# One block for load, first norm, router and first feed-forward, with the gate weights turned as bf16 parts

## The chip, the cores and the metric

The kernel runs on one core of a Trainium2 chip. The metric is the device time of one execution in microseconds (us); lower is better. The kernel before takes 1775.18 us in the median of three runs (1761.94, 1775.18 and 1776.92). One execution was taken with the hardware profiler; its own time is 1773.67 us.

## What is computed

Two transformer-like layers on x of 16 x 256 x 128 floats, 4096 rows (tokens) of 128. Only the first lines of it are touched here:

```python
xn = layernorm(x)
x = x + attn0(xn) + ffn0(xn)          # layer 0
...
# ffn0: 8 experts, hidden size 64 each (512 together), the two best experts per row
logits = xn @ router_w + router_b
w, idx = top_k(softmax(logits), 2); w = w / sum(w)
mask[row, idx] = w                                # 8 gate weights per row, six of them 0
h1 = gelu(einsum('btd,nde->btne', xn, W1) + b1)
out = sum over n of (einsum('btne,nef->btnf', h1, W2) + b2) * mask
```

`attn0` is a third-order linear attention with 16 heads of 64; layer 1 (norm, attention with relative positions, a capacity-limited expert layer) follows. Nothing of these is changed.

## The kernel before

The program is written engine by engine; each engine runs its list in order and waits on semaphores. A `Block` ends with a barrier of all five engines, so no instruction of a stage starts before the stage ahead has ended. Order is set by hand alone; there is no scheduler. The 4096 rows are 32 tiles of 128 (`NT`), taken in 8 groups of 4 tiles (`NG`, `TPG`, `GT` = 512 rows). `xnT_all` holds the normed rows turned, 128 features on the partitions.

Four stages touch the change, in this order:

1. `constants` (from line 76). POOL makes identity, masks and index rows; SP issues three loads (line 86): all of x as one transfer of 2 MB, and two router matrices.
2. `norm_stage` (from 114). DVE waits for all three loads, then takes the statistics of 32 tiles (line 151) in a loop, 9 small steps on 128x32 values, with a square root by ACT (186) between. Then a loop over pairs of groups: DVE norms 8 tiles (172), PE turns them (206), ACT copies the turned group out of PSUM (192), PE multiplies it with the router (212), POOL copies it to `xnT_all` (228), and DVE copies the logits (178). DVE norms the next pair only after it has copied this pair's logits.
3. `ffn0_stage` (from 282). After the barrier SP loads the feed-forward's weights (313 to 318); DVE, ACT and PE wait for all five. PE computes the first group's hidden values (379, one product of 512 columns for each of 4 chunks of 128 hidden units). DVE finds the two best experts of all rows (`top2_steps`, 249 to 274, and 332 to 341) in one chain on 128x256 values, each step waited for. Then 8 groups: ACT writes every gate weight 64 times beside each other (`wx`, 363), PE turns it once for the bias product (385) and 16 times for the four chunks (392), so that the PSUM tile `ps_w` holds each hidden unit's gate weight; ACT applies Gelu (369), DVE multiplies (347), PE computes the next group's hidden values (379) and then the outputs: for each tile 4 products with W2 (401) and one with b2 (403). DVE adds them to x (350).
4. `attn0_stage`: its first product is line 586.

A product with float32 operands is issued as two passes, so 4 products of line 379 are 8 rows in the trace; a transpose (206, 385, 392) is one.

## Time and profile before

| what | value |
|---|---|
| median of three runs | 1775.18 us |
| profiled execution, its own time | 1773.67 us |
| its span, first to last instruction | 1772.1 us |
| PE busy | 1612.4 us, 91% |
| granted TensorE clock, mean | 0.974 |
| start of the first product of `attn0_stage` | 181.59 us |

The profile page gives busy time by engine (PE is TensorE's matmuls, PEld its weight loads, DVE VectorE, ACT ScalarE, POOL GpSimd, SP the queue that issues the transfers), the span in 40 slices of 44.3 us, and groups of instructions. The timeline lists instructions in order of time, neighbours of one line merged. The windows view gives busy time and granted clock of chosen stretches. A duration is of one execution.

### The profile page before, as it was taken

To read this page: it belongs to the slowest core of one execution; us is meant where nothing else is said; L and a number is where in the kernel's file an instruction comes from. 1 tells how busy PE (TensorE), PEld (TensorE's weight loads), DVE (VectorE), ACT (ScalarE), POOL (GpSimd) and SP (SyncE) were. 2 spreads that over 40 slices of the span, in tenths; PEclk is the share of its full clock that TensorE was granted. 3 is DMA by queue.
4 is the path that set the end of the run, shared out by engine and by line. 5 is a ranking of instruction groups with operands and counts; after the bars stand their busy time and mean duration, and the time that the engine had idled before them with its cause. 6 is when DMAs were issued, how large, how long until landed. Compare 5 with 4: busy or idle time off the path is not lost. (4 is left out here: it accounts for less than half of the span.)

```text
span 1772.1 us, 39751 instructions
## 1 busy us (share of the span) xinstructions
PE 1612.4 (91%) x14552; PEld 1267.3 (72%) x14552; DVE 917.8 (52%) x3198; ACT 752.9 (42%) x2111; POOL 297.4 (17%) x377
## 2 busy tenths in 40 slices
PE   3599999999999999999959999977999999999995
PEld 3366788888888888888835656645777777777774
DVE  3322554545454545454532222225777777777774
ACT  1232122222222222222222222228887888887873
POOL 1000220010111111110052000001232233233222
PEclk9999899999999999999979999998999999999998
DMA  1200750000000000000024233218888888888886
GB/s 48 63 0 0 73 102 19 4 10 6 7 4 7 6 5 6 5 6 7 7 89 132 73 106 107 77 62 237 254 229 244 247 232 251 247 238 224 242 239 178
DMA packets 230781, 181.43 MB, mean 102 GB/s; under 512 B 82591, under 2 KB 219641, under 8 KB 230640
## 3 DMA queue, kind: packets, MB, share of 16 engines
q1 hardware_dynamic: 225266, 167.14, 35.0%
q0 software_dynamic: 5376, 12.44, 2.4%
q8 instruction: 87, 1.43, 0.3%
q14 instruction: 52, 0.43, 0.1%
HBM read 103.60 MB, written 75.78 MB: 101 GB/s over the span
## 5 line engine op out<-in xcount | busy, mean ns | idle before, releaser
L769 DVE TENSOR_TENSOR a0MT<-a0ps_M,mask 128x384 f32<-128x384 f32 x256 | 142.5, 557 | 223.2 <-PE a0ps_M L614 223.2
L1542 ACT ACTIVATE a1Pm<-a1Pm,a1nmx 128x256 f32<-128x256 f32 x512 | 255.7, 505 | 0.8 <-DVE a1nmx L1604 0.8
L1604 DVE CUSTOM_DVE_ANT_0 a1Pm<-a1ps_S,a1Sb 128x256 f32<-128x256 f32 x512 | 196.2, 420 | 88.6 <-issue 84.8
L722 ACT ACTIVATE a0oT<-a0ps_o 128x256 f32<-128x256 f32 x128 | 49.1, 383 | 441.3 <-PE a0ps_o L626 326.1
L1537 ACT ACTIVATE a1Rt<-a1ps_R 128x384 f32<-128x384 f32 x264 | 128.7, 487 | 113.1 <-PE a1ps_R L1402 93.5
L1421 PE MATMUL a1ps_T<-ident,a1Pm 128*128 128x128 f32 x1024 | 156.6, 275 | 0.0
L1157 DVE TENSOR_TENSOR f1hid<-f1ge,f1ps_b 128x512 f32<-128x512 f32 x80 | 54.9, 687 | 193.7 <-PE f1ps_b L1090 186.2
L612 PE MATMUL a0ps_M<-a0AT 128*128 128x256 f32 x512 | 153.7, 382 | 1.2 <-DVE a0AT L764 1.2
L764 DVE TENSOR_TENSOR a0AT<-a0ps_A,mask 128x384 f32<-128x384 f32 x256 | 130.8, 552 | 39.4 <-PE a0ps_A L595 39.4
L586 PE MATMUL a0ps_qk<-xnT_all,a0w_in 128*128 (+1 forms) x512 | 146.6, 409 | 1.4 <-PEq L310 1.4
L1402 PE MATMUL a1ps_R<-rel_st,a1stk 72*128 72x192 bf16 x528 | 90.0, 253 | 45.2 <-ACT a1Rt L1537 24.1
L712 ACT ACTIVATE a0qk<-a0ps_qk 128x512 f32<-128x512 f32 x128 | 76.3, 596 | 96.6 <-PE a0ps_qk L586 96.6
L1421 PEld LDWEIGHTS a1ps_T<-ident,a1Pm 128*128 128x128 f32 x1024 | 115.5, 142 | 0.4 <-issue 0.2
L586 PEld LDWEIGHTS a0ps_qk<-xnT_all,a0w_in 128*128 128x128 f32 x512 | 87.7, 191 | 30.3 <-issue 23.3
L613 PEld LDWEIGHTS a0ps_M<-a0AT 128*128 128x128 f32 x512 | 97.6, 191 | 13.3
L1100 PE MATMUL f1ps_o<-f1wo,f1hid 128*128 128x128 f32 x768 | 91.5, 280 | 15.4 <-DVE f1hid L1157 15.4
L1100 PEld LDWEIGHTS f1ps_o<-f1wo,f1hid 128*128 128x128 f32 x768 | 88.6, 195 | 19.5 <-DVE f1hid L1157 11.9
L1411 PE MATMUL a1ps_S<-a1stk 72*128 72x256 bf16 x512 | 101.3, 280 | 0.0
L1088 PE MATMUL f1ps_a<-f1xT,f1w 128*128 128x512 f32 x192 | 99.3, 599 | 0.7 <-ACT f1xT L1120 0.7
L1542 ACT ACTIVATION_READ_ACCUMULATOR a1Pm<-a1Pm,a1nmx 128x1 f32 x512 | 99.9, 195 | 0.0
L614 PE MATMUL a0ps_M<-a0AT 128*128 128x128 f32 x512 | 99.2, 276 | 0.0
L613 PE MATMUL a0ps_M<-a0AT 128*128 128x128 f32 x512 | 98.6, 274 | 0.0
(242 smaller groups left out, 3009.1 us busy)
## 6 DMA issues: line engine op xcount, KB each, us to landing
skew<-a1Rt SPq DMA_DIRECT2D x132, 384.0 KB, 5.3
a1Sb<-skew SPq DMA_DIRECT2D x131, 384.0 KB, 5.4
a1stk<-parts SPq DMA_DIRECT2D x153, 64.0 KB
a1stk<-parts SPq DMA_DIRECT2D x51, 192.0 KB
parts<-a1prt SPq DMA_DIRECT2D x18, 384.0 KB, 5.6
f1w<-in_L_ffn_w_kernel SPq DMA_DIRECT2D x16, 344.0 KB, 3.0
f1w<-in_L_ffn_w_kernel SPq DMA_DIRECT2D x16, 320.0 KB, 3.3
f1wo<-in_L_ffn_wo_kernel SPq DMA_DIRECT2D x16, 320.0 KB, 4.4
```

Source lines behind the costliest of these rows:

```text
L586: ins = nc.tensor.matmul(ps_qk[:, i, :], w_in[:, i, p * P:(p + 1) * P], xnT_all[:, bass.ds(b * T, T)], start=True, stop=True)
L612: nc.tensor.matmul(ps_M[h][:, 0:T], AT[h][:, 0:P], AT[h][:, 0:T], start=True, stop=True)
L613: nc.tensor.matmul(ps_M[h][:, T:HB], AT[h][:, P:T], AT[h][:, P:T], start=True, stop=False)
L764: nc.vector.tensor_tensor(AT[h][:, :], ps_A[h][:, 0:HB], mask[:, :], ALU.mult).then_inc(A_ready, 1)
L769: nc.vector.tensor_tensor(MT[i][h][:, :], ps_M[h][:, 0:HB], mask[:, :], ALU.mult).then_inc(M_ready, 1)
L1088: nc.tensor.matmul(ps_a[u % 2][:, :], w[i][:, u * P:(u + 1) * P], xT[i][:, :], start=True, stop=True).then_inc(a_done, 1)
L1100: ins = nc.tensor.matmul(ps_o[i][:, s, :], hid[:, c, s * P:(s + 1) * P], wo[i][:, c, :], start=(c == 0), stop=(c == HC - 1))
L1411: ins = nc.tensor.matmul(ps_S[hp % 2][:, n, :], stk[par][:, 0, h, it * P:(it + 1) * P], stk[par][:, 1, h, :], start=True, stop=True)
L1421: ins = nc.tensor.transpose(ps_T[k % 2][:, n, jt, :], Pm[:, place(2 * k + n), jt * P:(jt + 1) * P], ident[:, :])
L1537: nc.scalar.activation(Rt[:, hp, :, :], ps_R[:, :, :].rearrange("p n c -> p c n"), ACT.Copy).then_inc(sm["R_ready"], 1)
L1542: nc.scalar.activation(Pm[:, place(h), :], Pm[:, place(h), :], ACT.Exp, bias=nmx[it][:, h:h + 1], scale=-1.0, accum_out=den[it][:, h:h + 1 ...
L1604: nc.vector.tensor_tensor_reduce(out=Pm[:, place(h), :], in0=ps_S[hp % 2][:, n, :], in1=bias_of(it, hp, n), scale=-1.0, scalar=3.0e38, op0 ...
```

## The change

Four functions are replaced by one, `front_stage`, in one `Block`:

- x is loaded in four transfers of 8 tiles; the statistics of a quarter wait for that quarter alone. Routers, gate bias, b1, W1, W2 and b2 are issued right behind x by SP. b2 is loaded nine times into a cleared tile (three copies of 8 rows in each of three blocks of 32 partitions).
- All loops are written out. In the norm, the order on PE is: turn group g, then the router products of group g-1; ACT copies the turned group straight to `xnT_all`; the router's results of all 32 tiles stay in one PSUM tile. POOL has no part in it.
- Of the softmax only the difference of the two largest logits goes through exp; the two weights are 1/(1+e) and e/(1+e).
- DVE splits the gate weights into three bf16 parts (`pw`, 128 columns a tile), and b2 likewise (`b2s`). PE turns `pw` by a bf16 product with a bf16 identity (357), ACT copies the result as bf16 (`wT`, 318), and PE repeats each weight over its expert's hidden rows by one bf16 product of 512 columns per chunk with a 0/1 matrix `esel` (364). The bias product (375) is bf16 with all 128 rows.
- In a group PE does two repeats, two hidden products of the next group, two repeats, two hidden products, the turning of the next group's weights, and the outputs.

The float32 products with W1 and W2, Gelu, the multiplication by DVE and the addition to x stay.

```diff
-def constants(nc, ident, mask, iota_e, ltri, ones_bf, group_base, one, load, loaded):
...
-def norm_stage(nc, x_all, xn_all, xnT_all, ident, router, logits, tag, loaded=None, loads=0):
...
-def top2_steps(nc, v, done, soft, iota_e, m, tag, exp_start, exp_done):
...
-def ffn0_stage(nc, x_all, xnT_all, logits, router_b, W1, b1, W2, b2, ident, iota_e, attn_load, attn_loaded, load_tables):
...
+KPARTS = 3
...
+def front_stage(nc, a, x_all, xnT_all, ident, mask, iota_e, ltri, ones_bf, group_base, one, router, attn_load, attn_loaded, load_tables):
+    XL = 4
+    TPL = NT // XL
+    SMALL = 4 + KPARTS * KPARTS
...
+        pw = m.sb("f0pw", [P, NT, 4, P // 4], BF16)
+        wT = [m.sb(f"f0wT{i}", [P, GT], BF16) for i in range(2)]
...
+        ps_l = ps_y[:, :, :].rearrange("p j d -> p (j d)")[:, 0:NT * E].rearrange("p (t e) -> p t e", e=E)
+            @block.sync
+            def _(sp):
+                x_dram = a["L0_attn_x"].rearrange("b (t p) d -> p (b t) d", p=P)
+                for q in range(XL):
+                    sp.dma_start(x_all[:, q * TPL:(q + 1) * TPL, :], x_dram[:, q * TPL:(q + 1) * TPL, :]).then_inc(x_in[q], 16)
+                sp.dma_start(router[:, 0, :], a["L0_ffn_router_w"]).then_inc(small, 16)
+                sp.dma_start(router[:, 1, :], a["L1_ffn_router_w"]).then_inc(small, 16)
+                sp.dma_start(rb[:, :], a["L0_ffn_router_b"].partition_broadcast(P)).then_inc(small, 16)
+                sp.dma_start(b1c[:, :], a["L0_ffn_b1"].rearrange("(c e) f -> (e f) c", e=EPC), allow_slow_non_contiguous=True).then_inc(small, 16)
+                sp.dma_start(w1[:, :, :].rearrange("p c (e f) -> p (c e) f", e=EPC),
+                             a["L0_ffn_W1"].rearrange("e d f -> d e f")).then_inc(weights, 16)
+                sp.dma_start(w2[:, :, :], a["L0_ffn_W2"].rearrange("e f d -> (e f) d").rearrange("(c p) d -> p c d", p=P)).then_inc(weights, 16)
+                sp.wait_ge(b2_clear, 1)
+                for j in range(KPARTS):
+                    for k in range(KPARTS):
+                        sp.dma_start(b2f[j * 32 + k * E:j * 32 + (k + 1) * E, :], a["L0_ffn_b2"]).then_inc(small, 16)
+                for dst, src in attn_load:
+                    sp.dma_start(dst, src).then_inc(attn_loaded, 16)
+                load_tables(sp)
...
+                for k in range(KPARTS):
+                    pool.wait_ge(cs, 5 + k)
+                    nc.gpsimd.affine_select(out=esel[:, :, :, :], in_=esel[:, :, :, :], compare_op=ALU.not_equal, fill=1.0,
+                                            base=-E * k, pattern=[[-EPC, FC0], [-1, EPC], [0, FF0 // E]], channel_multiplier=1).then_inc(cs, 1)
+                nc.gpsimd.tensor_copy(ident_bf[:, :], ident[:, :]).then_inc(cs, 1)
...
+            @block.vector
+            def _(v):
+                def nstep(n, ins):
+                    ins.then_inc(norm_step, 1)
+                    v.wait_ge(norm_step, NT + n)
+                for q in range(XL):
+                    v.wait_ge(x_in[q], 16)
+                    for t in range(q * TPL, (q + 1) * TPL):
+                        nc.vector.bn_stats(stats[:, t:t + 1, :], x_all[:, t:t + 1, :]).then_inc(norm_step, 1)
+                v.wait_ge(norm_step, NT)
...
+                for g in range(NG):
+                    if g > 1:
+                        v.wait_ge(xT_done, g - 1)
+                    for j in range(TPG):
+                        t = g * TPG + j
+                        ins = nc.vector.tensor_scalar(xn[g % 2][:, j, :], x_all[:, t, :], mean[:, t:t + 1], rstd[:, t:t + 1],
+                                                      ALU.subtract, ALU.mult)
+                    ins.then_inc(xn_ready, 1)
+                v.wait_ge(small, 16 * SMALL)
+                nc.vector.tensor_copy(b2p[:, :], b2f[:, :]).then_inc(b2_step, 1)
+                v.wait_ge(b2_step, 1)
...
+                v.wait_ge(lg_done, NG)
+                v.wait_ge(cs, 4)
+                gstep(1, nc.vector.tensor_tensor(wt[:, :, :], ps_l, bc(rb[:, :], 1, NT), ALU.add))
+                src = wt
...
+                v.wait_ge(pw_clear, 1)
+                src = wt
+                for k in range(KPARTS):
+                    ins = nc.vector.tensor_copy(pw[:, :, 0:KPARTS, k * E:(k + 1) * E], bc(src[:, :, :], 2, KPARTS))
+                    if k < KPARTS - 1:
+                        gstep(19 + 2 * k, ins)
+                        gstep(20 + 2 * k, nc.vector.tensor_tensor(rest[:, :, :], src[:, :, :], pw[:, :, 0, k * E:(k + 1) * E], ALU.subtract))
+                        src = rest
+                    else:
+                        ins.then_inc(pw_ready, 1)
...
+                act.wait_ge(small, 16 * SMALL)
+                def keep_h(g, c):
+                    act.wait_ge(h_done, g * FC0 + c + 1)
+                    if g > 0:
+                        act.wait_ge(hw_ready, (g - 1) * FC0 + c + 1)
+                    nc.scalar.activation(h[:, c, :], ps_h[c][:, :], ACT.Gelu, bias=b1c[:, c:c + 1]).then_inc(h_ready, 1)
+                def keep_wT(g):
+                    act.wait_ge(wT_done, g + 1)
+                    if g > 1:
+                        act.wait_ge(y_done, g - 1)
+                    nc.scalar.activation(wT[g % 2][:, :], ps_g[:, :], ACT.Copy).then_inc(wT_kept, 1)
+                for c in range(FC0):
+                    keep_h(0, c)
+                keep_wT(0)
+                for g in range(NG):
+                    if g < NG - 1:
+                        for c in range(FC0):
+                            keep_h(g + 1, c)
+                        keep_wT(g + 1)
+            @block.tensor
+            def _(pe):
+                def turn_x(g):
+                    pe.wait_ge(xn_ready, g + 1)
+                    if g > 1:
+                        pe.wait_ge(xT_ready, g - 1)
+                    for j in range(TPG):
+                        ins = nc.tensor.transpose(ps_w[g % 2][:, j * P:(j + 1) * P], xn[g % 2][:, j, :], ident[:, :])
+                    ins.then_inc(xT_done, 1)
+                def route(g):
+                    pe.wait_ge(xT_ready, g + 1)
+                    for j in range(TPG):
+                        t = g * TPG + j
+                        ins = nc.tensor.matmul(ps_l[:, t, :], xnT_all[:, t * P:(t + 1) * P], router[:, 0, :], start=True, stop=True)
+                    ins.then_inc(lg_done, 1)
+                def hidden(g, cs):
+                    for c in cs:
+                        if g > 0:
+                            pe.wait_ge(h_ready, (g - 1) * FC0 + c + 1)
+                        nc.tensor.matmul(ps_h[c][:, :], w1[:, c, :], xnT_all[:, g * GT:(g + 1) * GT], start=True, stop=True).then_inc(h_done, 1)
+                def turn_weights(g):
+                    if g > 0:
+                        pe.wait_ge(wT_kept, g)
+                    for j in range(TPG):
+                        parts = pw[:, g * TPG + j, :, :].rearrange("p j c -> p (j c)")
+                        ins = nc.tensor.matmul(ps_g[:, j * P:(j + 1) * P], parts, ident_bf[:, :], start=True, stop=True)
+                    ins.then_inc(wT_done, 1)
+                def repeat_weights(g, cs):
+                    for c in cs:
+                        if c >= 2 or g > 0:
+                            pe.wait_ge(hw_ready, g * FC0 + c - 1)
+                        nc.tensor.matmul(ps_w[c % 2][:, :], esel[:, c, :, :].rearrange("p e f -> p (e f)"), wT[g % 2][:, :],
+                                         start=True, stop=True).then_inc(w_done, 1)
+                def outputs(g):
+                    pe.wait_ge(hw_ready, (g + 1) * FC0)
+                    if g > 0:
+                        pe.wait_ge(y_added, g)
+                    for j in range(TPG):
+                        rows = slice(j * P, (j + 1) * P)
+                        for c in range(FC0):
+                            nc.tensor.matmul(ps_y[:, j, :], hw[:, c, rows], w2[:, c, :], start=(c == 0), stop=False)
+                        ins = nc.tensor.matmul(ps_y[:, j, :], wT[g % 2][:, rows], b2s[:, :], start=False, stop=True)
+                    ins.then_inc(y_done, 1)
+                pe.wait_ge(cs, 3)
+                for g in range(NG):
+                    turn_x(g)
+                    if g == 1:
+                        pe.wait_ge(small, 16 * SMALL)
+                    if g > 0:
+                        route(g - 1)
+                route(NG - 1)
+                pe.wait_ge(weights, 16 * 2)
+                hidden(0, range(FC0))
+                pe.wait_ge(cs, 9)
+                pe.wait_ge(pw_ready, 1)
+                turn_weights(0)
+                pe.wait_ge(b2_step, 2 * KPARTS)
+                for g in range(NG):
+                    pe.wait_ge(wT_kept, g + 1)
+                    repeat_weights(g, (0, 1))
+                    if g < NG - 1:
+                        hidden(g + 1, (0, 1))
+                    repeat_weights(g, (2, 3))
+                    if g < NG - 1:
+                        hidden(g + 1, (2, 3))
+                        turn_weights(g + 1)
+                    outputs(g)
```

The order on PE in the norm. Before (names ending in 0 and 1 are the two buffers), the loop's body, run three times after a first copy of it:

```order
L206 MATMUL n0ps_t0<-ident,n0xn0 128x128 x4
L204 REGISTER_ALU
L206 MATMUL n0ps_t1<-ident,n0xn1 128x128 x4
L212 MATMUL n0ps_l0<-router,n0xT0 128x8 x4
L212 MATMUL n0ps_l1<-router,n0xT1 128x8 x4
L72 REGISTER_ALU
L72 COMPARE_AND_BRANCH
```

After, the start of the list:

```order
L336 MATMUL f0ps_w0<-ident,n0xn0 128x128 x4
L336 MATMUL f0ps_w1<-ident,n0xn1 128x128 x4
L343 MATMUL f0ps_y<-router,xnT_all 128x8 x4
L336 MATMUL f0ps_w0<-ident,n0xn0 128x128 x4
L343 MATMUL f0ps_y<-router,xnT_all 128x8 x4
L336 MATMUL f0ps_w1<-ident,n0xn1 128x128 x4
```

Between the turning of a group and its router products now stands the turning of the next.

One group of the feed-forward on PE. Before, the loop's body:

```order
L385 MATMUL f0ps_t<-ident,f0wx 8x128 x4
L392 MATMUL f0ps_w<-ident,f0wx 128x128 x8
L389 ISA
L392 MATMUL f0ps_w<-ident,f0wx 128x128 x4
L389 REGISTER_ALU
L392 MATMUL f0ps_w<-ident,f0wx 128x128 x4
L378 REGISTER_ALU
L379 ISA
L379 MATMUL f0ps_h<-xnT_all,f0w 128x512 x4
L401 MATMUL f0ps_y<-f0w,f0hw 128x128 x4
L403 MATMUL f0ps_y<-f0b,f0wT 128x128
```

After:

```order
L364 MATMUL f0ps_w<-f0wT,f0esel 128x512 x2
L350 MATMUL f0ps_h<-xnT_all,f0w 128x512 x2
L364 MATMUL f0ps_w<-f0wT,f0esel 128x512 x2
L350 MATMUL f0ps_h<-xnT_all,f0w 128x512 x2
L357 MATMUL f0ps_g<-f0ident_bf,f0pw 128x128 x4
L374 MATMUL f0ps_y<-f0w,f0hw 128x128 x4
L375 MATMUL f0ps_y<-f0b2s,f0wT 128x128
```

Four products of 512 columns stand in the place of 20 transposes, and the hidden products stand between them. The last two rows come four times in both.

## Rows read from the trace of the kernel before

**Rows 1.** Page: busy time of each engine and its share of the span.
```profile
PE 1612.4 (91%) x14552; PEld 1267.3 (72%) x14552; DVE 917.8 (52%) x3198; ACT 752.9 (42%) x2111; POOL 297.4 (17%) x377
```
**Rows 2.** Windows, stretch by stretch: length, busy us (instructions) by engine, clock, DMA.
```profile
0.00:22.21 22.21, 0.00 (x0) 0.00 (x0) 9.51 (x42) 1.51 (x2) 2.82 (x17) 1.00 0.35 95
22.21:51.62 29.41, 21.50 (x96) 19.68 (x96) 10.37 (x40) 4.78 (x8) 4.87 (x8) 1.00 0.00 0
51.62:57.48 5.86, 0.00 (x0) 0.00 (x0) 0.01 (x1) 1.28 (x1) 0.00 (x0) 1.00 0.63 157
57.48:69.66 12.18, 5.41 (x8) 2.08 (x8) 10.69 (x29) 0.42 (x1) 0.00 (x0) 0.92 0.52 150
69.66:86.50 16.84, 13.19 (x69) 9.49 (x70) 2.57 (x4) 8.11 (x8) 0.00 (x0) 0.85 0.01 4
86.50:164.99 78.49, 71.92 (x410) 51.44 (x409) 19.55 (x30) 28.63 (x36) 0.00 (x0) 1.00 0.00 0
164.99:181.59 16.60, 13.25 (x62) 10.73 (x61) 3.95 (x6) 2.86 (x5) 0.03 (x1) 0.66 0.00 0
280.00:880.00 600.00, 600.00 (x4548) 511.15 (x4548) 308.56 (x911) 147.32 (x369) 56.87 (x76) 1.00 0.02 6
```
**Rows 3.** Timeline of a pair of groups in the norm: start, us, engine, line.
```profile
37.13 2.24 DVE L172 TENSOR_SCALAR n0xn<-x_all,n0mean,n0rstd 128x128 f32 x8 [0.59 <-issue]
38.39 2.15 PE L206 MATMUL n0ps_t<-ident,n0xn 128*128 128x128 f32 x8 [2.19 <-DVE n0xn L172]
40.19 3.48 PEld L212 LDWEIGHTS n0ps_l<-router,n0xT 128*128 128x128 f32 x16
```
**Rows 4.** Timeline: the last load of the feed-forward and the wait for it.
```profile
54.14 0.63 SPq L318 DMA_DIRECT2D f0b<-in_L_ffn_b  x1
57.48 0.42 DVE L332 TENSOR_TENSOR f0wt<-logits,f0rb 128x256 f32<-128x256 f32 x1 [5.86 <-DMA f0b<-in_L_ffn_b]
57.94 0.42 DVE L249 TENSOR_REDUCE f0mx<-f0wt 128x32 f32<-128x256 f32 x1
```
**Rows 5.** Timeline: eight of the first group's transposes.
```profile
72.23 1.72 PEld L392 LDWEIGHTS f0ps_w<-ident,f0wx 128*128 128x128 f32 x8
```
**Rows 6.** Windows by clock level, columns as in rows 2.
```profile
57.50:60.90 3.40, 3.40 (x4) 1.51 (x5) 2.75 (x7) 0.42 (x1) 0.00 (x0) 1.00 1.02 381
67.80:74.60 6.80, 2.73 (x12) 2.09 (x12) 1.64 (x5) 3.79 (x4) 0.00 (x0) 0.50 0.11 20
74.70:170.20 95.50, 85.60 (x488) 61.38 (x489) 25.38 (x39) 35.71 (x46) 0.00 (x0) 1.00 0.00 0
```
**Rows 7.** Timeline of a group in the steady part, and of the last.
```profile
155.57 3.68 PE L379 MATMUL f0ps_h<-xnT_all,f0w 128*128 x8
160.48 1.16 PE L401 MATMUL f0ps_y<-f0w,f0hw 128*128 128x128 f32 x8
161.57 0.48 PE L403 MATMUL f0ps_y<-f0b,f0wT 8*128 8x128 f32 x2
174.71 2.08 PE L401 MATMUL f0ps_y<-f0w,f0hw 128*128 128x128 f32 x8
176.71 0.79 PE L403 MATMUL f0ps_y<-f0b,f0wT 8*128 8x128 f32 x2
```
**Rows 8.** Timeline of the start.
```profile
1.95 5.89 SPq L86 DMA_DIRECT2D router<-in_L_ffn_router_w  x2
11.70 1.96 DVE L151 BATCH_NORM_STATS2 n0stats<-x_all  x8 [11.70 <-DMA router<-in_L_ffn_router_w]
20.10 0.21 DVE L154 TENSOR_TENSOR n0mean<-n0stats 128x32 f32<-128x32 f32 x1
```
**Rows 9.** Groups by line: a cast from float32 to bf16 on DVE.
```profile
L884 DVE CAST t1parts<-t1rpad 8x384 bf16<-8x384 f32 x1 | 0.3, 348 | 0.0
```
**Rows 10.** Timeline: bf16 products of the later attention, 256 columns each.
```profile
1501.43 0.39 PE L1411 MATMUL a1ps_S<-a1stk 72*128 72x256 bf16 x2
1501.66 0.33 PE L1402 MATMUL a1ps_R<-rel_st,a1stk 72*128 72x192 bf16 x2
```

More of the change, by code:

```diff
@@ L1837, in program @@
                 mask = g.sb("mask", [P, T + P])
-                logits = g.sb("logits0", [P, NT, E])
-                x_dram = a["L0_attn_x"].rearrange("b (t p) d -> p (b t) d", p=P)
-                load = [(x_all[:, :, :], x_dram), (router[:, 0, :], a["L0_ffn_router_w"]), (router[:, 1, :], a["L1_ffn_router_w"])]
-                x_loaded = g.sem("x_loaded")
                 w_in0 = g.sb("a0w_in", [P, 3, H0 * DK])
@@ L1844, in program @@
                 w_loaded = g.sem("a0loaded")
-                constants(nc, ident, mask, iota_e, ltri, ones_bf, group_base, one, load, x_loaded)
-                norm_stage(nc, x_all, None, xnT_all, ident, router[:, 0, :], logits, "n0", x_loaded, len(load))
                 attn_load = [(w_in0[:, i, :], a["L0_attn_W_" + n]) for i, n in enumerate("qkv")]
                 attn_load.append((w_out0[:, :, :], a["L0_attn_W_o"].rearrange("(c p) d -> p c d", p=P)))
-                ffn0_stage(nc, x_all, xnT_all, logits, a["L0_ffn_router_b"], a["L0_ffn_W1"], a["L0_ffn_b1"], a["L0_ffn_W2"],
-                           a["L0_ffn_b2"], ident, iota_e,
-                           attn_load, w_loaded, load_tables)
+                front_stage(nc, a, x_all, xnT_all, ident, mask, iota_e, ltri, ones_bf, group_base, one, router, attn_load, w_loaded,
+                            load_tables)
                 attn0_stage(nc, a, x_all, xnT_all, xn_all, w_in0, w_out0, w_loaded, mask, one, zeros, ident, router[:, 1, :], iota_e, ltri,
```

414 lines of the change are left out of this document (132 added, 282 removed).

## The prediction

> **What bounds the kernel now.** The page comes first: PE is busy for 91% of the span [rows 1], but this share is a mean over stages, so the second view is the table of stretches [rows 2]. In it a reader is to see two different kernels. From 280 to 880 us, in the first attention, PE is busy for all of 600 us: what starts this stage earlier ends it earlier. The stretch ahead of it, up to 181.59 us, is the one that the change rewrites, and there PE is busy for about 125 us (the sum of its column). So the change is priced by the time at which line 586 starts, and nothing behind that line is expected to move by itself.
>
> The stretches also say what waits. For 22.21 us PE does nothing: a load, statistics, small steps. In 22.21 to 51.62 the norm holds every engine below 75%: the four pairs of groups take 7.35 us each [rows 2], made of 1.26 us of DVE alone (37.13 to 38.39), 2.15 us of transposes and 3.48 us of router products, and the next pair starts only behind them [rows 3]. Then 5.86 us of waiting for the feed-forward's loads [rows 4], 12.18 us of gating on DVE, 16.84 us for the first group, 78.49 us for six groups (13.08 each) with PE busy for 92%, and 16.60 us for the last group and the barrier [rows 2].
>
> **The clock on the way.** The clock column reads 1.00 in the norm, but the durations don't: 16 router passes take 3.48 us, 0.218 each [rows 3], as the transposes do at 72.23, 8 in 1.72 us or 0.215 each, in a stretch granted 0.50 [rows 5, 6]. In the stretch at 1.00 an output pass takes 0.136 (8 from 160.48 to 161.57) [rows 6, 7]. I read the norm as run at the lower level (1.2 GHz), and take the column there as not recorded (it reads 1.00 from 57.50 to 60.90 too, with passes of 0.85 us [rows 6]).
>
> **Start to first normed tile: 22.21 us before, 15.8 after.** The statistics waited for all of x and two routers until 11.70; the last began 0.5 us before the steps at 20.10, so 32 took 8.4 us [rows 8]. In quarters, three quarters of them hide under the transfer. The last quarter lands at 11.7 at the latest, and its 8 take 1.96 us. The small steps, 20.10 to 22.21, stay 2.1 us: fewer waits, same chain through ACT. Sum 15.8.
>
> **Norm and router, up to the gating's first step: 57.48 before, 39.0 after.** PE starts 1.26 us behind DVE as before. A group costs it 4 transposes at 0.215 and 8 router passes at 0.218, 2.6 us; DVE needs 1.1 us for a group (half of 2.24), ACT 0.6 (4.78 us for 8) [rows 2, 3], and both now work under PE, since the turning of the next group stands between. Eight groups: 20.8 us. POOL's copies and DVE's logits copies go; none of them was late, so they count as nothing.
> PE's first router product now waits for all 13 small loads. Before, SP's two router transfers, issued behind x, occupied it until 7.84 [rows 8]. Behind them stand four others of 0.33 to 0.57 us and nine of b2; one of b2 took 0.63 [rows 4], so nine take 6.1 us at that price and the last is issued at 15.8. Before, the last load landed 2.7 us behind its issue (54.77 to 57.48) [rows 4]: 18.5. PE asks for it at 15.8 + 1.26 + 1.7 = 18.8. I charge 1 us of waiting; zero is the lower end, and the upper end is the second rival. The load wait of 5.86 us is gone, and b2's splitting (9 DVE steps near 0.2 us) lies under the last two groups of PE. Sum 15.8 + 1.26 + 20.8 + 1.0 + 0.1 = 39.0; gain 18.5.
>
> **Gating: 12.18 before, 10.5 after.** Steps of 128x256 follow each other in 0.46 us (57.48, 57.94) [rows 4]. The new chain has 17 of them, about 1.0 us of 128x32 steps, and three casts of 768 elements. A cast of 384 took 0.348 [rows 9] and a step of 256 0.42; a cast of 768 lies between 0.5 (by the cast's slope) and 0.95 (by twice a step of 384 without its start-up). I take 0.55, the cast being the nearest row. 7.8 + 1.0 + 1.65 = 10.5, gain 1.7; with the upper end 0.5. ACT's exp lies under four DVE steps. The first hidden products lie under the gating, as before.
>
> **First group: 16.84 before, 12.9 after.** Turning and copying the weights: about 0.5 for four bf16 products, 0.6 for the copy (ACT's 128x512 copies in the norm) [rows 2], hops 0.3: 1.4 in place of 1.9 us for `wx` and what follows it. PE has then been idle and starts at the lower level: two repeats near 0.43 each, four hidden passes at 0.85 (4 in 3.40 us from 57.50 on) [rows 6]: 4.3. The clock then rose both times after about 3 us of unbroken work, 57.50 to 60.9 and 71.6 to 74.6 [rows 6]. The rest at the upper level, 7.2 (next part). Gain 3.9.
>
> **Six groups: 78.5 before, 56.5 after.** At the upper level eight hidden passes take 3.68 us with the tail of the last, 0.43 each or 3.44 [rows 7]. The outputs cost 1.09 us for 8 passes of line 401 (160.48 to 161.57) and about 0.41 for the two of line 403 (0.48 with the tail), 1.5 a tile, 6.0 a group. The bf16 bias product is one pass. Two bf16 products of 256 columns begin and give way in 0.23 us [rows 10], so 512 columns cost 0.23, with 0.86 (two float32 passes) as the upper end; the bias product of 128 columns I put at 0.1, between 0.06 and 0.41 likewise. So: repeats 0.92, hidden 3.44, turning 0.3, outputs 4 x 1.19 = 4.76; 9.4 a group. The 20 transposes and PE's waits for DVE go; the window of six groups holds 6.6 us of idle PE, 1.1 a group [rows 2]. Nothing takes their place: DVE needs 3.3 us a group (19.55 us in six) [rows 2] and ACT 3.0 (five steps of 0.6), and the hidden products stand where PE waited. Their cover is wide: DVE's four multiplications (0.65 each in the same window) end about 0.4 us ahead of the outputs. Gain 22.0.
>
> **Last group and barrier: 16.60 before, 13.4 after.** No hidden products to hide DVE: its addition and four multiplications, 3.7 us. Before, the clock fell in this group, and a tile of outputs took 2.0 us for eight passes (174.71 to 176.71) and 0.7 for two [rows 7]. I expect that again: 2.0 + 0.15 for a tile, 8.3 in all (the first tile partly at the upper level), and the same 1.4 us to line 586. Gain 3.2.
>
> **Sum.** 18.5 + 1.7 + 3.9 + 22.0 + 3.2 = 49.3 us. Line 586 moves from 181.6 to 132.3. Against the profiled execution's own 1773.7: **1724 us**. That execution is 1.5 us below the median of the three runs, which differ by 15 us among themselves.
>
> **Rivals.**
> *The clock rises in the norm.* Its PE list is now unbroken. Against: in each pair before, 5.6 us without a gap (2.15 of transposes, then 3.48 of router passes of 8 columns) didn't raise it [rows 3], whereas 2.8 us of mostly transposes at 71.6 did [rows 6]; so router passes seem to count for little, and they are two thirds of the new list. For: the pairs had a gap of 2 us, the new list has none. It would save half of what is left after some 4 us, 8.4 us, but DVE's 1.1 us a group then sets the pace: gain 57, 1717 us.
> The Trainium skill ("TensorE: Matmul & The Clock Gate", section "What's actually happening") says that the clock follows how busy PE has recently been and does not count instructions. By that rule this rival is the forecast, at 1717; the pairs of the norm speak against it as far as they go.
>
> *The nine loads of b2 hold SP.* The two router transfers took 2.9 us each on SP with x in flight [rows 8]. At that price nine take 26.5 us, 20 more than charged, and all of it falls on PE, which has only two groups to turn before it waits: gain 29, 1745 us. Against: x has landed at 11.7, and the queue should be free after that; so at worst a part.
>
> *The clock stays low through the feed-forward.* This ends above the time before. At the lower level a group costs 4 x 0.43 + 8 x 0.85 + 0.45 + 4 x 2.15 = 17.6 us in place of 9.4: six groups lose 49, the first group's second half 7; gain 49 - 56, 1781 us. It decides from about six groups at that level. It would need PE to look less busy with single-pass products of 0/1 weights than with transposes. Against: with gaps of over 1 us a group it was granted 1.00 for 95.5 us without a break [rows 6], and the new list has fewer.
>
> *Written-out code is read late*, or the longer chains meet a wait not seen here: no row shows a stall of this kind; it belongs to the small remainder.
>
> **Chances.** Forecast 0.62, clock in the norm 0.19, loads 0.13, low clock 0.04, unnamed 0.02. The range reaches from the first rival, less some spread of runs, to most of the second: **1709 to 1740 us**. A measurement of this kernel can tell about 1% (18 us). Faster by more: 0.62 + 0.19 + 0.13 = 0.94. The low clock ends half within 1% and half above, with half of the unnamed each: 0.03 and 0.03.
>
> **What would show it.** The first product of the attention near 132 us. Normed tiles from 15.8 us; one group of the norm every 2.6 us on PE (1.1 to 1.3 if the clock rises). No wait of PE for a load over 1 to 2 us. From the last router product to the turning of weights 10.5 us. Groups every 9.4 us without a wait of PE; one of 17 would be the low clock. From line 586 on, the same 1590.5 us as before (1772.1 - 181.6). I am wrong if groups take over 11 us at full clock, since then the bf16 products cost what float32 ones do, or if the rest of the span gives back part of the gain.

## The result, and the profile after

The changed kernel takes 1711.03 us in the median of four runs (1698.71 to 1715.68); the kernel before 1773.51 (four runs). The ratio is 0.9647, with a 95% interval of 0.9587 to 0.9706: 3.5% faster. The profiled execution took 1715.68 us, its span is 1714.1, 58.0 us less than before. The forecast was 1724 (1709 to 1740).

The page's busy row, to be read against [rows 1]: TensorE's work fell by 28 us, the span by 58, so half of the gain is idle time.

```profile
span 1714.1 us, 39121 instructions
PE 1584.3 (92%) x14424; PEld 1247.7 (73%) x14424; DVE 920.5 (54%) x3193; ACT 741.9 (43%) x2103; POOL 299.4 (17%) x376
```

The windows of the changed kernel, cut where its stages change: start; norm and router; gating; first group; six groups; last group and barrier. Columns as in [rows 2], whose stretches they answer to.

```profile
0.00:14.40 14.40, 0.00 (x0) 0.00 (x0) 7.96 (x41) 1.51 (x2) 9.19 (x24) 1.00 0.78 186
14.40:35.83 21.43, 20.17 (x97) 19.77 (x98) 10.48 (x41) 6.06 (x9) 0.00 (x0) 1.00 0.37 107
35.83:46.29 10.46, 5.13 (x8) 1.88 (x8) 9.62 (x24) 3.94 (x6) 0.00 (x0) 0.98 0.00 0
46.29:58.58 12.29, 11.48 (x55) 7.27 (x56) 2.57 (x4) 3.83 (x6) 0.00 (x0) 0.74 0.00 0
58.58:109.76 51.18, 51.18 (x314) 36.60 (x312) 19.01 (x30) 19.42 (x30) 0.00 (x0) 1.00 0.00 1
109.76:120.32 10.56, 7.28 (x43) 5.86 (x41) 3.81 (x6) 0.00 (x0) 0.01 (x1) 0.84 0.00 0
```

The last window ends at 120.32, where attention's first product starts (line 568 now). The reader is to see that TensorE is busy without a gap for the six groups (51.18 of 51.18 us, before 71.92 of 78.49). It is idle where VectorE's chain stands alone (the start, 5.4 us of the gating, 2.0 us of the last group), for 0.8 us behind ScalarE's first copy of the weights, and for 1.3 us at the barrier. The timeline of TensorE shows one group of the norm, and most of a steady group (start, us, line):

```profile
19.22 1.09 PE L336 MATMUL f0ps_w<-ident,n0xn 128*128 128x128 f32 x4
20.11 1.71 PE L343 MATMUL f0ps_y<-router,xnT_all 128*128 128x8 f32 x8
...
58.64 0.59 PE L364 MATMUL f0ps_w<-f0wT,f0esel 128*128 128x512 bf16 x2
59.07 1.88 PE L350 MATMUL f0ps_h<-xnT_all,f0w 128*128 128x512 f32 x4
60.79 0.59 PE L364 MATMUL f0ps_w<-f0wT,f0esel 128*128 128x512 bf16 x2
61.22 1.88 PE L350 MATMUL f0ps_h<-xnT_all,f0w 128*128 128x512 f32 x4
62.94 0.39 PE L357 MATMUL f0ps_g<-f0ident_bf,f0pw 128*128 128x128 bf16 x4
63.16 1.11 PE L374 MATMUL f0ps_y<-f0w,f0hw 128*128 128x128 f32 x8
64.11 0.22 PE L375 MATMUL f0ps_y<-f0b2s,f0wT 128*128 128x128 bf16 x1
64.16 1.11 PE L374 MATMUL f0ps_y<-f0w,f0hw 128*128 128x128 f32 x8
```

Start to start, a group of the norm is 2.45 us (19.22 to 21.67); an output tile is 1.00 us (63.16 to 64.16), of which 0.95 are the eight float32 passes and 0.05 the bf16 bias product. In the kernel before the same tile took 1.50 [rows 7].

Behind 120.32 not all is as it was. From attention's first product to the end the changed kernel takes 1593.8 us (1714.1 - 120.32), the one before 1590.5. By stage, before and after: first attention 730.4 and 739.0, second feed-forward 277.7 and 275.1, second attention 582.5 and 579.7. (A stage is counted from its first product to that of the next; the second feed-forward's is the transpose that waits for its gathered rows, the second attention's the first that reads `a1stk`.) So 61.3 us were won ahead of the attention and 3.3 given back. The experiments take up both.

### The profile page after: what moved, and what is told of

Same layout as the page of the kernel before. It is cut to its first block and busy times, and to the rows that moved or that the text cites. A ratio compares the mean times of both kernels' runs of the same rounds, so it can differ in the third digit from the quotient of the medians.

```text
span 1714.1 us, 39121 instructions
## 1 busy us (share of the span) xinstructions
PE 1584.3 (92%) x14424; PEld 1247.7 (73%) x14424; DVE 920.5 (54%) x3193; ACT 741.9 (43%) x2103; POOL 299.4 (17%) x376
```

## The experiments

Each is one profiled execution, unless a number of runs is named. Since whole spans scatter, verdicts rest on when attention starts and on stage lengths. The first four cut the change into parts. In a diff, `...` stands for lines left out.

**The kernel before with its bias product over 128 rows.**

```diff
-        b2s = m.sb("f0b2", [E, D])
+        b2s = m.sb("f0b2", [P, D])
-        wT = m.sb("f0wT", [E, GT])
+        wT = m.sb("f0wT", [P, GT])
...
+                nc.gpsimd.memset(b2s[:, :], 0.0).then_inc(padded, 1)
+                nc.gpsimd.memset(wT[:, :], 0.0).then_inc(padded, 1)
...
```

> The kernel before, with one edit: wT and b2s have 128 rows instead of 8, cleared once, so that the bias product contracts over 128 partitions, still in float32; the result is the same. Theory A (the number of rows): a float32 product over 8 rows keeps the weight loads of its neighbours from running under it, and that is what made a tile of outputs cost 1.50 us against the 1.00 after the change. Then a tile costs about 1.07 us (ten passes at 0.107), a steady group 13.08 - 1.7 = 11.4 us, and the attention starts near 167 instead of 181.6. Theory B (the type): float32 passes next to each other cost 0.136 and a bf16 product between them is what made the others cheap. Then a tile stays at 1.5 us and the attention starts at 181.6.

Measured: attention starts at 167.33 us, where theory A had it, 14.3 earlier than in the kernel before; 1752.81 us. Its timeline, an output tile:

```profile
103.90 1.05 PE L409 MATMUL f0ps_y<-f0w,f0hw 128*128 128x128 f32 x8
104.79 0.39 PE L411 MATMUL f0ps_y<-f0b,f0wT 128*128 128x128 f32 x2
105.01 1.06 PE L409 MATMUL f0ps_y<-f0w,f0hw 128*128 128x128 f32 x8
```

A tile falls from 1.50 to 1.11 us with the same number of passes and more data: the bias product takes 0.22 in place of 0.41 (start to start), and the eight passes behind it 0.89 in place of 1.09. The 8-row product cost twice, once itself and once in its neighbours. This is what the forecast of the output tiles lacked. A steady group takes 11.64 us (92.26 to 103.90) in place of 13.08, so eight groups account for 11.5 of the 14.3 us. In the last group the clock fell later (1.00 up to 160 us, 0.77 from there to 167.3; before, 0.50 to 0.52 from 170 us to attention's start); what this part is worth was not separated.

**The changed kernel with float32 transposes and an 8-row float32 bias product, as before, in place of the bf16 parts.**

```diff
-                        ins = nc.tensor.matmul(ps_g[:, j * P:(j + 1) * P], parts, ident_bf[:, :], start=True, stop=True)
+                        ins = nc.tensor.transpose(ps_g[0:E, j * P:(j + 1) * P], wx[:, j, :, 0], ident[:, :])
...
-                        nc.tensor.matmul(ps_w[c % 2][:, :], esel[:, c, :, :].rearrange("p e f -> p (e f)"), wT[g % 2][:, :],
-                                         start=True, stop=True).then_inc(w_done, 1)
+                        for j in range(TPG):
+                            wide = wx[:, j, c * EPC:(c + 1) * EPC, :].rearrange("p e f -> p (e f)")
+                            ins = nc.tensor.transpose(ps_w[c % 2][:, j * P:(j + 1) * P], wide, ident[:, :])
+                        ins.then_inc(w_done, 1)
```

> The changed kernel with the bf16 parts undone: ACT widens the gate weights, PE turns them by 4 + 16 float32 transposes a group, and the bias product is float32 over 8 rows; block, loads, order and written-out loops stay. Theory A (the gain of a group is the sum of its parts): transposes 2.1 us, hidden products 3.44, outputs 6.0: 11.6 us a steady group; the gating is 2.7 us shorter without the casts; the attention starts near 143. Theory B (ACT's widening of 1.9 us comes onto the path): 12.5 to 13 us a group, near 151.

Measured: attention at 138.88 us, 1724.88 us. That is earlier than either theory gave, though the group is theory A's (11.6 us). The timeline of a group:

```profile
65.36 1.16 PE L375 MATMUL f0ps_y<-f0w,f0hw 128*128 128x128 f32 x8
66.45 0.48 PE L376 MATMUL f0ps_y<-f0b2e,f0wT 8*128 8x128 f32 x2
...
69.87 0.61 PE L356 MATMUL f0ps_g<-ident,f0wx 128*8 128x128 f32 x4
70.31 1.04 PE L365 MATMUL f0ps_w<-ident,f0wx 128*128 128x128 f32 x8
```

A group is 11.53 us against 8.53, and TensorE has no gap in it either. Of the 3.0 us, 1.9 are the four output tiles (5.90 for 4.01), and 1.1 the 20 transposes (0.44 and twice 0.88) in place of 1.08 us of bf16 products. So the bf16 parts are worth 18.6 us (138.88 - 120.32) at this place. Two thirds of a group's share come from the new bias product: by the run before, about 1.6 us from its 128 rows in place of 8 (0.39 a tile), the rest from one bf16 pass in place of two float32 ones. One third comes from fewer passes for turning and repeating.

**The changed kernel with each group's hidden products behind all four repeats, not between them.**

```diff
-                    repeat_weights(g, (0, 1))
+                    repeat_weights(g, (0, 1, 2, 3))
                     if g < NG - 1:
-                        hidden(g + 1, (0, 1))
-                    repeat_weights(g, (2, 3))
-                    if g < NG - 1:
-                        hidden(g + 1, (2, 3))
+                        hidden(g + 1, (0, 1, 2, 3))
```

> The changed kernel with one part undone: all four repeats first, then all four hidden products of the next group, as before the change. Theory A (the order is worth PE's waits): PE waits for DVE between the repeats again, 1.1 to 1.3 us a group; a steady group takes 8.53 + 1.2 = 9.7 us and the attention starts near 129 instead of 120.3. Theory B (the waits were hidden by something else): 8.5 us a group, 120 to 121.

Measured: attention at 128.22 us, 7.9 later, as theory A said; 1713.67 us. TensorE waits twice in a group, for the two PSUM tiles that VectorE still reads, and a group is 10.0 us (69.40 to 79.44). The order between the repeats is worth about 8 us.

```profile
69.40 0.38 PE L364 MATMUL f0ps_w<-f0wT,f0esel 128*128 128x512 bf16 x1
70.73 0.39 PE L364 MATMUL f0ps_w<-f0wT,f0esel 128*128 128x512 bf16 x1 [0.95 <-DVE f0hw L291]
71.33 0.39 PE L364 MATMUL f0ps_w<-f0wT,f0esel 128*128 128x512 bf16 x1 [0.21 <-DVE f0hw L291]
```

**The changed kernel with x in one transfer.**

```diff
-                for q in range(XL):
-                    sp.dma_start(x_all[:, q * TPL:(q + 1) * TPL, :], x_dram[:, q * TPL:(q + 1) * TPL, :]).then_inc(x_in[q], 16)
+                sp.dma_start(x_all[:, :, :], x_dram[:, :, :]).then_inc(x_in[0], 16)
...
```

> The changed kernel with x loaded by one transfer again; the statistics wait for all of it. Theory A (the quarters hide three quarters of the statistics): these start near 11 us instead of 5.35; 24 of them at 0.206 us, 4.9 us, come onto the path; the first tile is normed near 19.5 instead of 14.4 and the attention starts near 125.5. Theory B (the small transfers or the routers set the start): 14.4 to 15.5 and 120.3 to 121.5.

Measured: attention at 125.43 us, 5.1 later, as theory A said; 1720.44 us. The statistics (VectorE's timeline) start when all of x is there; in the changed kernel half of them are done by 8.8 us:

```profile
11.49 6.28 DVE L216 BATCH_NORM_STATS2 n0stats<-x_all 128x6 f32<-128x128 f32 x32 [11.49 <-DMA x_all<-in_L_attn_x]
```

```profile
5.35 3.43 DVE L217 BATCH_NORM_STATS2 n0stats<-x_all 128x6 f32<-128x128 f32 x16 [5.35 <-DMA x_all<-in_L_attn_x]
8.96 1.64 DVE L217 BATCH_NORM_STATS2 n0stats<-x_all 128x6 f32<-128x128 f32 x8 [0.18 <-DMA x_all<-in_L_attn_x]
10.94 1.65 DVE L217 BATCH_NORM_STATS2 n0stats<-x_all 128x6 f32<-128x128 f32 x8 [0.34 <-DMA x_all<-in_L_attn_x]
```

**The clock in the norm: 24 products that nobody reads, ahead of it.**

```diff
+                def filler(n, bank):
+                    for _ in range(n):
+                        nc.tensor.matmul(bank[:, :], fill[:, 0:P], fill[:, :], start=True, stop=True)
...
+                pe.wait_ge(x_in[2], 16)
+                filler(24, ps_h[0])
```

> The changed kernel with 24 bf16 products of 512 columns on TensorE, read by nobody, between the landing of the third quarter of x (about 9 us) and the first transpose of the norm (15.7 us). They should raise the clock before the norm begins. Theory A, that the clock follows how busy TensorE's rows are and falls again because a group's 32 router passes write 8 columns each: the first one to three groups of the norm take about 1.5 us, the rest 2.45 us as before, attention begins at 116 to 121 us (120.3 without the change). Theory B, that it stays where it is as long as TensorE has no gap: all eight groups run at VectorE's 1.3 us each (10.48 us busy over 8), the norm ends 9 us earlier, attention begins near 111 us.

Measured: attention at 111.35 us, 9.0 earlier, where theory B had it, but not quite for its reason; 1701.54 us. TensorE's timeline:

```profile
19.33 0.64 PE L339 MATMUL f0ps_w<-ident,n0xn 128*128 128x128 f32 x4
19.80 0.96 PE L346 MATMUL f0ps_y<-router,xnT_all 128*128 128x8 f32 x8
...
24.93 2.72 PE L346 MATMUL f0ps_y<-router,xnT_all 128*128 128x8 f32 x16
27.51 6.18 PE L353 MATMUL f0ps_h<-xnT_all,f0w 128*128 128x512 f32 x8
```

A group takes 1.28 us, TensorE's own work at 2.4 GHz, in place of 2.45. At 25 us the granted clock falls (1.00 from 20 to 25 us, 0.65 from 25.0 to 27.5), and TensorE's last gap, of 0.20 us, lies 8 us back. So the norm of the changed kernel did run at 1.2 GHz, as its durations said and the clock column (1.00) did not. And the fall within unbroken work speaks against theory B, by which the clock stays as long as TensorE has no gap, as six groups at the higher clock speak against theory A's one to three. A later run, of the two edits further down with 24 such products of 480 columns, lost it at 23.2 us (windows):

```profile
15.82:23.20 7.38, 7.14 (x65) 6.81 (x64) 6.78 (x27) 3.59 (x6) 0.00 (x0) 1.00 0.78 240
23.20:29.79 6.59, 6.59 (x34) 6.59 (x34) 2.27 (x12) 2.48 (x4) 0.00 (x0) 0.51 0.15 26
```

Both stretches have TensorE busy to over 96% with transposes and router passes, one at 1.00, the next at 0.51. What sets the moment of the fall is open.

**The same, and two more such products after each group of the norm.**

```diff
+                    filler(2, ps_h[1])
```

> As the run with 24 products ahead of the norm, and two more such products after each group of the norm. If columns streamed per group are what holds the clock (theory A), two products (0.43 us of 1.8 at the higher clock) may hold it up: 8 groups at 1.3 to 1.8 us, the norm and router some 14 us long in place of 21.4, attention near 113 us. If they are too few, each costs 0.43 us at the lower clock: the norm gets 7 us longer, attention begins near 127 us. Theory B of the run before: same as that run, plus 3.5 us, near 114.5 us.

Measured: the clock stays at 1.00 through the norm and the eight hidden passes behind it (3.68 us in place of 6.18); a group takes 1.68 us; attention at 113.77, where theory A had it; 1706.92 us. TensorE's timeline, the last full group and the hidden passes:

```profile
25.05 0.60 PE L339 MATMUL f0ps_w<-ident,n0xn 128*128 128x128 f32 x4
...
26.72 0.60 PE L339 MATMUL f0ps_w<-ident,n0xn 128*128 128x128 f32 x4
...
29.21 3.68 PE L353 MATMUL f0ps_h<-xnT_all,f0w 128*128 128x512 f32 x8
```

With two products of 512 columns a group, the clock stayed in this one run; with 8-column passes and transposes alone it fell in all three. The products cost 0.4 us a group, and the run before had lost the clock only near the norm's end. So its router products end 1.7 us sooner (its hidden passes start at 27.51, these at 29.21), and so does attention start sooner there.

**What was given back: GpSimd's two table subtractions, moved out of the attention.** In the changed kernel's timeline, GpSimd and VectorE at the start of attention:

```profile
121.03 8.82 POOL L542 TENSOR_TENSOR t1rvd<-t1rv 1x4088 f32<-1x4088 f32 x1
185.82 8.82 POOL L542 TENSOR_TENSOR t1rvd<-t1rv 1x4088 f32<-1x4088 f32 x1 [55.98 <-DMA rv_table<-t1rvd]
```

```profile
124.12 5.80 DVE L861 TENSOR_SCALAR t1rpad<-t1rk 8x129 f32<-8x129 f32 x1
129.96 0.28 DVE L862 TENSOR_SCALAR t1rpad<-t1rk 8x129 f32<-8x129 f32 x1
...
186.94 7.74 DVE L765 TENSOR_TENSOR n1dif<-n1stats 128x2 f32<-128x2 f32 x1
194.59 0.15 DVE L766 TENSOR_TENSOR n1m<-n1stats 128x2 f32<-128x2 f32 x1
```

Both long VectorE instructions end when GpSimd's do (129.9 and 194.6), and their twins right behind take 0.28 and 0.15 us. The view of waits from 120 to 240 us (total, times, longest) shows what it costs TensorE, which needs VectorE's masks; and the windows, that the clock is low behind each wait:

```profile
PE a0ps_M L594 <- DVE a0AT L746: 7.3, 2, 4.1
```

```profile
131.00:138.00 7.00, 6.19 (x26) 4.88 (x28) 3.75 (x10) 0.00 (x0) 0.00 (x0) 0.51 0.80 87
196.00:203.00 7.00, 6.20 (x26) 4.95 (x28) 4.32 (x12) 0.63 (x2) 0.02 (x1) 0.51 0.45 112
```

```diff
+                nc.gpsimd.tensor_tensor(tin.rvd[:, :, :], tin.rv[:, :, :], tin.rv[:, TAB - 1:TAB, :].to_broadcast([1, TAB, HD]),
+                                        ALU.subtract).then_inc(rvd_made, 1)
+                pool.wait_ge(rvd_out, 16)
+                nc.gpsimd.tensor_tensor(tin.rvd[:, :, :], tin.rv[:, :, :], tin.rv[:, 0:1, :].to_broadcast([1, TAB, HD]),
+                                        ALU.subtract).then_inc(rvd_made, 1)
```

(in `front_stage`, behind gating, with SP's two transfers of the table; both are gone from `attn0_stage`)

> The changed kernel with GpSimd's two one-partition subtractions of the value tables (8.8 us each, at 121 and 185.8 us, both inside attention) moved into the feed-forward's block, behind gating. Theory A, that such an operation holds VectorE's scalar and small-tensor instructions until it ends: VectorE's rpad step takes 0.3 us in place of 5.8 and n1dif 0.15 in place of 7.7, TensorE's waits of 3.1 and 4.1 us for them go, with the stretches at the lower clock behind them; attention from its first product to the second feed-forward takes 727 to 731 us in place of 739, and the kernel ends near 1706 us. In the feed-forward the same operation may lengthen VectorE's instructions in its place, but those that read PSUM with large tiles should hold nothing up for over 1 us in sum. Theory B, that VectorE was late for its own work and only ended at the same time by chance: attention takes 739 us as before and the time stays at 1714 to 1716 us.

Measured: the first attention takes 724.4 us in place of 739.0, both of TensorE's waits and both falls of the clock are gone; 1701.6 us. The first held instruction is back at its own time (VectorE's timeline):

```profile
124.03 0.27 DVE L867 TENSOR_SCALAR t1rpad<-t1rk 8x129 f32<-8x129 f32 x1
```

Theory A, and by more than it said. In their new place (46.30 and 56.87, 8.8 us each) they hold nothing up: VectorE's multiplications there, which read PSUM, keep 0.64 us each.

The 14.6 us are two things, and other profiles tell them apart. Three of the runs above left the subtractions in the attention and reached it at full clock: the padded bias product, the hidden products behind the repeats, and the 24 products ahead of the norm. Their VectorE was held in the same way, and TensorE waited the same 3.14 us, but there the clock did not fall behind the wait. TensorE's timeline, first in the changed kernel, then in the run with 24 products:

```profile
131.81 1.22 PE L594 MATMUL a0ps_M<-a0AT 128*128 128x256 f32 x2 [3.14 <-DVE a0AT L746]
```

```profile
122.83 0.70 PE L604 MATMUL a0ps_M<-a0AT 128*128 128x256 f32 x2 [3.14 <-DVE a0AT L756]
```

| profiles | TensorE's waits for held masks, us | granted clock behind them | first attention, us |
|---|---|---|---|
| changed kernel (two profiles, the second further down), x in one transfer, two more products a group | 6.8 to 7.5 | falls, twice | 736.5 to 739.8 |
| padded bias product, hidden products behind, 24 products ahead of the norm | 4.7 to 4.9 | 1.00 | 729.4 to 730.4 |
| tables moved (four profiles, with those further down) | none | 1.00 where they were | 724.4 to 725.9 |

The run with float32 transposes fits the middle row: its clock was partly low at attention's start (0.80 and 0.77 in the first 8 us), it waited 3.3 us for the masks and took 730.3. So the hold alone costs some 5 us, and the falls of the clock behind it some 8 more, where they come. They came in four of the seven profiles of the first two rows, with the same list of attention's instructions; why in these is open.

In the kernel before the first subtraction stood at 182.27 and held VectorE for 4.10 us, but its attention took only 730.4 us. Its last group had left TensorE at 1.2 GHz, so it reached the held mask later and didn't wait for it; at the second subtraction it waited 1.2 us. VectorE's timeline and the windows:

```profile
187.06 4.10 DVE L879 TENSOR_SCALAR t1rpad<-t1rk 8x129 f32<-8x129 f32 x1
```

```profile
181.60:188.00 6.40, 5.71 (x18) 4.07 (x19) 2.92 (x6) 0.60 (x1) 6.40 (x3) 0.50 0.49 54
```

Against 724.4, the kernel before lost 6.0 us here, to the low clock up to 190 us and to that wait, and the changed kernel 14.6, to the hold and to the clock behind it. The difference, 8.6, is the length that attention gained; the two later stages were 5.4 us shorter, which leaves the 3.3 given back.

**The changed kernel, and the one with the tables moved, five runs each.**

> The changed kernel once more, unedited, for the scatter of its time: its four executions so far gave 1698.71 to 1715.68 us. If the hold of VectorE by GpSimd sometimes ends with TensorE's clock falling behind it and sometimes not, the executions fall into two heaps, near 1700 and near 1714 us; the median between 1707 and 1714. Its profiled attention takes 726 to 731 us where the clock stays up at 131 and 196 us, and 736 to 739 where it falls.

> The changed kernel with GpSimd's two table subtractions moved into the feed-forward's block, timed five times beside the unedited one. Theory A (the hold costs TensorE 3.1 and 4.1 us of waiting, and sometimes the clock behind it): all executions near 1701 us, median 5 to 11 us below the unedited kernel's, with less scatter. Theory B (its one run was a lucky one): scatter and median as the unedited kernel's, within 2 us.

Measured: unedited, a median of 1711.41 us (1708.28 to 1714.69), ratio to before 0.9654, interval 0.9629 to 0.9679; its five times form no two heaps. Tables moved, 1701.56 (1696.72 to 1708.87), ratio 0.9611, interval 0.9584 to 0.9638. The first attention takes 739.8 us in the one profile and 725.6 in the other. The stage gain of 14 us came back; of it 10 us show in the median. Some of the unedited kernel's executions may have kept the clock up behind the waits, as three profiles above did; no run shows it, since stages are known for the profiled execution alone. The scatter did not shrink (12.2 us from lowest to highest, against 6.4), so theory A was wrong there.

**All together, to look for the fastest.** Tables moved, 24 products of 480 columns ahead of the norm, 12 in the wait for gating, 4 and 4 in the last group's waits; and a second kernel with the first two of these edits alone:

```diff
+                filler(24, ps_h[0])
...
                 hidden(0, range(FC0))
+                filler(12, ps_w[0])
...
+                    if g == NG - 1:
+                        filler(4, ps_h[0])
                     repeat_weights(g, (2, 3))
+                    if g == NG - 1:
+                        filler(4, ps_h[0])
```

> The changed kernel with both edits that worked apart, and two more: 24 products ahead of the norm; GpSimd's two table subtractions in the feed-forward's block; 12 bf16 products of 480 columns in TensorE's wait for gating (4.5 us), and 4 in each of the two waits for VectorE in the last group (0.95 and 0.85 us). Theory A, that the two gains stand at different places and add up: attention at 111.4 us by the first edit, its length 724 to 728 us by the second, and the rest 855 us: span near 1691 us. The products in gating keep the clock up into the first group (11.5 us there, 8.5 in a steady group: up to 2.5 us less), those in the last group spare its stretch at the lower clock (up to 1.7 us): attention near 108 us, the kernel at 1687 to 1690 us. Theory B, that the clock falls somewhere later all the same and takes back what was won: 1696 to 1702 us, no better than either edit alone.

> The run before without the 12 and the 4 and 4 products: only the 24 products ahead of the norm and the two table subtractions moved. Theory A: attention at 111.4 us and a span of 1690 to 1694 us; the difference to the run before, 2 to 4 us at attention's start, is what the clock costs in the first and the last group. Theory B: attention at 111.4 us, a span of 1698 us or more.

Measured: all together 1701.79 us in the median of five (1698.71 to 1702.40), ratio 0.9604, interval 0.9575 to 0.9632; the two edits alone 1699.16 in one run. Attention starts at 114.87 and 113.05 us, not at 108 and 111.4, since the clock fell earlier in the norm (21.2 and 23.2 us); the products in gating brought nothing in the first group (11.5 us long, as in the run with 24 products alone; 12.3 in the changed kernel), and in the last group it stayed up without them too. With all edits it fell in attention's first products instead (0.50 from 118 to 120 us). Theory A's sum fails: attention starts 5 us earlier than with the tables alone (114.87 against 120.06) and the median is the same. In the profiles the second attention takes 581.3 and 582.9 us in these two, 577.0 and 574.2 in the two with the tables alone. An earlier start alone doesn't make that stage longer: it took 582.5 us in the kernel before, whose attention starts at 181.6, and 575.0 in the run with two products a group, at 113.8. What moves it by 9 us is open. The version to keep is the one with the tables moved.

## Why the prediction was right, and where it was off

The median was 13 us below the forecast and 2 us above the lower end of the range (the profiled execution, 8 us below the forecast). The mechanism was the forecast's: all the gain arose ahead of line 586. But attention started 12 us earlier than forecast, and that the time still lies inside the range is in part luck: the first attention took 8.6 us more, and with the tables moved the median was 1701.56, outside. Its steps, in us:

| step | forecast | measured |
|---|---|---|
| start to first normed tile | 15.8 | 14.40 |
| norm and router, with the load wait | 23.2 | 21.43 |
| gating | 10.5 | 10.46 |
| first group | 12.9 | 12.29 |
| six groups | 56.5 | 51.18 |
| last group and barrier | 13.4 | 10.56 |
| attention starts | 132.3 | 120.32 |
| from there to the end | 1590.5 | 1593.8 |

- *Start.* The last quarter of x landed at 10.94, not at 11.7, and a tile's statistics took 0.206 us written out, 0.24 in the loop.
- *Norm.* 2.6 us a group forecast, 2.45 measured, and TensorE waited for no load. The nine b2 transfers took SP 3.15 us in all, where the forecast had 6.1 from one row and its second rival 26.5. That rival is refuted.
- *Clock.* The first rival didn't come: 20 us of unbroken work, 64% of it router passes, raised nothing. The Trainium skill ("TensorE: Matmul & The Clock Gate", section "What's actually happening") says that the clock follows how busy TensorE has recently been; read so that any busy time counts, it would have made the forecast 1717. The trace disagrees with that reading: these 20 us stayed at 1.2 GHz, and a norm at 2.4 GHz lost the clock while TensorE was busy. 1717 would have been nearer to the time than 1724, but for a reason that isn't there.
- *Gating.* Right to 0.1 us. The cast of 768 elements was put at 0.55 and took 0.56.
- *Six groups.* This term was mis-sized most: 9.4 us a group forecast, 8.53 measured. The step that was off is "outputs 4 x 1.19". The step took the eight float32 passes at 1.09 us from a row in which an 8-row product stood between the tiles, and changed only that product's own price. The first experiment shows that the product slows the eight behind it: 0.89 without it. Four tiles at 1.00 are 0.75 us a group less, 4.5 of the term's 5.3 us.
- *Last group.* The clock was expected low for all tiles and fell for about 3.4 us only; in four other runs it didn't fall in this group.
- *Low clock in the feed-forward.* The rival on the other side didn't come: 1.00 for all six groups.
- *Behind line 586.* "The same 1590.5" was wrong by 3.3 us on balance, and by 8.6 in the first attention. The text had named this as a way to be wrong, without a mechanism. A TensorE that arrives at full clock runs into GpSimd's hold on VectorE, but that alone gives the old length (729.4 to 730.4 us in three profiles, where the kernel before lost as much to its low clock). The 8.6 us are the clock's falls behind the held waits, which four of seven profiles show.

## What to carry to other kernels

Price a group of instructions from a row in which its neighbours are those of the new list: here a product with few rows slowed what stood behind it, and a wait could leave the clock low for what followed. When a stage begins at another moment or clock, look at which fixed work of other engines (here two 8.8 us instructions on one partition) it now meets, and put such work beside instructions that it is seen not to hold. A clock column of 1.00 is believed only where the durations agree with it.

## What the runs showed of the hardware

- A float32 product over 8 rows among products over 128 costs about 0.4 us more than one over 128 rows with zeros in 120 of them: 0.2 in itself and 0.2 in the eight passes behind. No run here tells why.
- A GpSimd subtraction on one partition (4088 elements, 8.8 us) held a VectorE scalar instruction (0.28 us alone) for 5.80 and a 128x2 subtraction (0.15 alone) for 7.74 us, while VectorE instructions with one operand in PSUM kept their time. The Trainium skill ("SBUF — State Buffer", section "Who interferes with whom") says that the two engines share a pair of ports as an exclusive lock, which a VectorE instruction takes in its two-port modes or with two SBUF inputs, and that whoever issues first keeps the other out. The trace agrees, with GpSimd as the one that holds: the subtraction with two SBUF inputs was held, those with an operand in PSUM were not. That the scalar instruction ran in a two-port mode the trace doesn't show.
- TensorE at 2.4 GHz kept its clock through 5 to 10 us of transposes and 8-column passes and then lost it at 21.2, 23.2 and 25 us in three runs of that order, the last gap (0.20 to 0.34 us) being 3 to 8 us back; with two 512-column products per group it kept it (one run). Without products ahead, 20 us of the same work stayed at 1.2 GHz.
- Behind a wait of 3.14 us at the same place in the same instructions, TensorE's clock fell to 0.50 in four profiles and stayed at 1.00 in three.
